# Column tiles of 32 for all full products of a two-layer attention and expert kernel, with a new order of steps

## The chip, the cores and the metric

The kernel runs on one core of one Trainium2 chip. The metric is the device time of one execution in microseconds (us), the median over several runs. In the trace TensorE's work is shown as PE (products) and PEld (weight loads), VectorE as DVE, ScalarE as ACT, GpSimd as POOL and SyncE as SP.

## The reference

The input is x, 4 batches x 512 tokens x 128 channels, f32. Two layers follow, each with attention of 16 heads of 8 channels and a mixture of 8 experts:

```python
xn = _layernorm(x, axis=-1)
x = x + _L0_attn_ref(xn, ...) + _L0_ffn_ref(xn, ...)      # causal attention; block_fwd: norm, causal attention, norm, 8 experts
xn = _layernorm(x, axis=-1)
x = x + _L1_attn_ref(xn, ...) + _L1_ffn_ref(xn, ...)      # attention without a mask; top-2 of 8 experts
```

So each batch has three attentions (0 and 1 causal, 2 without a mask). The expert part of layer 0 sends all 512 tokens through all 8 experts (128 to 512 channels, GELU, 512 to 128) and weights the results with the gates, zero outside the top two. That of layer 1 has experts 128 to 128 to 128.

## The kernel before

A batch is handled as 4 tiles of 128 tokens. Activations live turned as well (`normed_T_*`, channels on partitions, 512 tokens in the free dimension). PSUM has 8 banks of 128 x 512 f32: seven are handed out to steps, the eighth (`sum_bank`) sums the heads.

All engines follow one list of steps. `SCORE` is a string of letters, each the next step of a chain (A: load, norms, turns and projections; F, G: norms and gates around the experts; K: filling the stacks; L: expert weights; M: row maxima; T: turn of the maxima; S: scores; V: values; H: heads; E and O: experts of layer 0, in and out; I and J: those of layer 1), and a digit behind a letter is the PSUM bank of that step. `plan` turns it into the list, and each engine's block goes through the list and issues what it has to do for a step, with semaphores between engines. So the string sets the order on every engine and on every DMA queue at once. Three queues take DMAs: SyncE's (most), ScalarE's and GpSimd's (parts of the first stacks).

An attention runs like this. `project` makes queries and keys, which are split into three bf16 parts; `stack` copies the parts by DMA into `q_stack` and `k_stack`, two slots each. A `max` step (L877, with L882 adding the causal mask) multiplies a 64-row half of the stack for two heads at a time, two products side by side in 64-row tiles of the array (form `64*128` in the trace), and VectorE takes the negated maximum of each row (L535). `max_turn` (L890) turns the maxima with TensorE, VectorE copies them (L545), and a DMA (L1159) puts them into the stack. A `scores` step (L904, also `64*128`) makes the scores turned, ScalarE exponentiates them (L778), GpSimd cuts the causal triangle (L1071), and `values` (L925) multiplies with the values: four products side by side, each with 32 output rows (form `128*32`).

All other products use the full array (`128*128`): `project` (L854, L857), `out_project` (L935), `route` (L945, 8 columns), `expert_in` (L973, 512 columns), `expert_out` (L986, 128 columns), and the turns of f32 tiles by TensorE's transpose (L841). The bias product `route_bias` (L960) has 8 rows. The trace shows each f32 product as two products with a weight load each; an order of the program lists it once. The last pieces of the first stack (attention 0 of batch 0) are issued by GpSimd; the first `max` step waits for them. `load_experts` (L1117) brings a quarter of the expert weights in two DMAs of 512 KB.

## Time and profile before

| | |
|---|---|
| runs | 742.81, 741.61, 742.12 us; median 742.12 |
| profiled execution | 742.59 us, its span 740.0 us |
| granted TensorE clock, mean | 0.987 |
| PE busy | 711.5 us, 96%, 6222 products |
| PEld busy | 387.6 us, 52% |
| DVE busy | 569.5 us, 77% |
| ACT busy | 509.3 us, 69%; 63 table loads in the steps, 1.28 us each |
| POOL busy | 185.2 us, 25% |
| expert weights | DMAs of 512 KB, 4.9 and 6.7 us to landing |

The span is the time from the first to the last instruction of the program; some 2.6 us of an execution lie around it. Products are pipelined, so a row's duration is longer than the distance to the next start; how long TensorE is held by a group is read from the start of the group to the start of the next one.

### The profile page before, as it was taken

The numbers are of one execution on the slowest core, as the hardware profiler recorded it, in microseconds if no ns is written. First come the engines' busy times: TensorE is split into PE (matmuls) and PEld (weight loads), VectorE is DVE, ScalarE is ACT, GpSimd is POOL, SyncE is SP. The second block draws the span as 40 slices with busy tenths as digits, with TensorE's granted clock in tenths as the row PEclk, the third lists the DMA queues.
The fourth block names the chain that finished last, engine by engine and source line by source line (L and its number), as shares of the span: only waits on it lengthen the run. The fifth ranks groups of instructions, "written<-read, shape, count | busy, mean of one in ns | idle before, by whom it ended". The sixth has DMA issues, their size and how long they took to land.

```text
span 740.0 us, 15886 instructions
## 1 busy us (share of the span) xinstructions
PE 711.5 (96%) x6222; PEld 387.6 (52%) x6222; DVE 569.5 (77%) x1127; ACT 509.3 (69%) x632; POOL 185.2 (25%) x425
## 2 busy tenths in 40 slices
PE   5689999999999999999999999999999999999997
PEld 2333345667645665564544456567654666533345
DVE  5989998545788868688999967658778476788966
ACT  7266777366686567667789866764787748588882
POOL 5165546011343012103533200021372110010000
PEclk9699999999999999999999999999999999999999
DMA  6243523000132000004232200031031000030101
GB/s 155 53 140 129 164 93 110 11 19 1 34 96 79 3 25 17 19 5 111 64 88 69 62 3 19 4 99 31 5 93 54 9 11 17 3 94 13 28 25 39
DMA packets 42009, 38.75 MB, mean 52 GB/s; under 512 B 14312, under 2 KB 37232, under 8 KB 41712
## 3 DMA queue, kind: packets, MB, share of 16 engines
q1 hardware_dynamic: 40592, 36.17, 17.5%
q10 hardware_dynamic: 1152, 1.05, 0.6%
q8 instruction: 49, 0.80, 0.5%
q0 software_dynamic: 192, 0.52, 0.3%
q14 instruction: 24, 0.20, 0.1%
HBM read 10.47 MB, written 1.44 MB: 16 GB/s over the span
## 4 chain that ended last, share of the span: by engine, by line
PE 79%; DVE 9%; ACT 4%; DMA 4%; issue 2%; POOL 1%; SPq 1%; ACTq 1%; POOLq 0%; DVEq 0%
PE psum L986 19%; PE psum L973 18%; PE psum L925 15%; PE psum L904 8%; PE psum L877 8%; DVE neg_max L535 6%; PE psum L854 2%; PE psum L935 1%; PE psum L882 1%; DMA inverses<-heads_den 1%; PE psum L857 1%; PE psum L945 1%; PE psum L960 1%; ACT k_stack L716 1%; DVE acc L690 1%
## 5 line engine op out<-in xcount | busy, mean ns | idle before, releaser
L535 DVE TENSOR_REDUCE neg_max<-psum 128x2 f32<-128x1024 f32 (+2 forms) x320 | 344.9, 1113 | 82.2 <-PE psum L877 40.2
L778 ACT ACTIVATE probs<-psum 128x1024 f32<-128x1024 f32 (+1 forms) x320 | 287.1, 938 | 122.4 <-PE psum L904 120.7
L802 ACT ACTIVATE probs<-psum,col 128x512 f32<-128x512 f32 x160 | 100.5, 684 | 78.9 <-PE psum L973 78.3
L925 PE MATMUL psum<-probs,v_ones 128*32 128x512 f32 (+3 forms) x1536 | 152.8, 496 | 0.1
L986 PEld LDWEIGHTS psum<-ew,probs 128*128 128x128 f32 x1024 | 120.1, 192 | 17.6 <-issue 14.2
L986 PE MATMUL psum<-ew,probs 128*128 128x128 f32 x1024 | 129.1, 280 | 0.0
L877 PE MATMUL psum<-k_stack,q_stack 64*128 64x512 bf16 (+3 forms) x768 | 113.7, 333 | 13.6 <-DMA q_stack<-part 8.2
L1071 POOL TENSOR_SCALAR_AFFINE_SELECT probs<-probs 128x512 f32<-128x512 f32 x128 | 82.0, 646 | 176.7 <-ACT probs L778 176.6
L973 PE MATMUL psum<-normed_T_a,ew 128*128 128x512 f32 x256 | 118.0, 599 | 0.0
L904 PE MATMUL psum<-q_stack,k_stack 64*128 64x512 bf16 (+3 forms) x768 | 109.2, 330 | 3.9 <-DVE neg_max L535 1.2
L690 DVE SCALAR_TENSOR_TENSOR acc<-psum,gate,acc 128x128 f32<-128x128 f32 x256 | 71.9, 344 | 23.5 <-PE psum L986 21.7
L1057 POOL CAST max_part<-neg_max 128x16 bf16<-128x16 f32 x48 | 9.8, 205 | 298.2 <-DVE neg_max L535 282.8
L730 ACT ACT_TABLE_LOAD x63 | 80.8, 1283 | 1.1
L877 PEld LDWEIGHTS psum<-k_stack,q_stack 64*128 64x128 bf16 x768 | 36.5, 94 | 76.3 <-issue 24.8
L904 PEld LDWEIGHTS psum<-q_stack,k_stack 64*128 64x128 bf16 x768 | 31.7, 94 | 75.9 <-ACT probs L778 28.4
L973 PEld LDWEIGHTS psum<-normed_T_a,ew 128*128 128x128 f32 x256 | 45.6, 190 | 48.0 <-issue 42.9
L925 PEld LDWEIGHTS psum<-probs,v_ones 128*32 128x32 f32 x1536 | 35.8, 108 | 48.5 <-issue 33.2
L882 PEld LDWEIGHTS psum<-above,pick 64*128 64x128 bf16 x1024 | 44.9, 97 | 16.9 <-issue 1.4
L882 PE MATMUL psum<-above,pick 64*128 64x64 bf16 x1024 | 52.4, 193 | 0.0
L986 PEld LDWEIGHTS psum<-wout,probs 128*128 128x128 f32 x256 | 31.1, 191 | 8.2 <-issue 5.2
L986 PE MATMUL psum<-wout,probs 128*128 128x128 f32 x256 | 35.1, 282 | 0.0
L1040 POOL TENSOR_TENSOR part<-rest,part 128x512 bf16<-128x512 f32 x24 | 27.4, 1157 | 12.8 <-ACT part L759 11.6
(124 smaller groups left out, 494.2 us busy)
## 6 DMA issues: line engine op xcount, KB each, us to landing
q_stack<-part SPq DMA_DIRECT2D x66, 128.0 KB, 2.4
k_stack<-part SPq DMA_DIRECT2D x66, 128.0 KB, 2.4
heads_raw<-head_sums SPq DMA_DIRECT2D x24, 128.0 KB
heads_inv<-inverses SPq DMA_DIRECT2D x12, 256.0 KB, 3.3
ew<-w_expert_in SPq DMA_DIRECT2D x4, 512.0 KB, 4.9
ew<-w_expert_out SPq DMA_DIRECT2D x4, 512.0 KB, 6.7
q_stack<-k_stack SPq DMA_DIRECT2D x14, 128.0 KB, 2.3
q_stack<-maxT SPq DMA_DIRECT2D x48, 32.0 KB, 1.8
```

Of the source, the lines that this page charges most:

```text
L535: eng.tensor_reduce(neg_max[:, q % 2, :, xs[0]:xs[-1] + 1, i], src, AX_X, ALU.max, negate=True).then_inc(vector_done.sem, 1)
L690: eng.scalar_tensor_tensor(out=acc_of[b % 2][:, t, :], in0=src[:, t * P:(t + 1) * P], scalar=gate_of[layer][:, t, expert:expert + 1], in1= ...
L730: eng.preload_act_table(table)
L778: eng.activation(dst, src, ACT.Exp, scale=SCALE).then_inc(probs_ready.sem, 1)
L802: ins = eng.activation(probs[:, order.slot[step[:-1]], 2 * k + f, :], two_banks(step)[:, f, :], ACT.Gelu_apprx_tanh if layer else ACT.Gelu ...
L877: ins = eng.matmul(dst[:, a, col0:col0 + keys], q_stack[slot][rows_of, head, i * P:(i + 1) * P], k_stack[slot][rows_of, head, 0:keys], sta ...
L882: ins = eng.matmul(dst[:, a, col0:col0 + HALF], pick[rows_of, upper, :], above[rows_of, upper, :], start=False, stop=upper == 1)
L904: ins = eng.matmul(dst[:, a, n * width:(n + 1) * width], k_stack[slot][rows_of, head, j * P:(j + 1) * P], q_stack[slot][rows_of, head, TIL ...
L925: ins = eng.matmul(sum_bank[32 * c:32 * c + V_COLS, q0:TILES * P], v_ones[u][:, j, g // 2 * QH + c, col0:col0 + V_COLS], probs[:, order.sl ...
L973: ins = eng.matmul(dst[:, f, :], w, normed_T["y" if layer else "a"][:, :], start=True, stop=True)
L986: ins = eng.matmul(dst[:, t * P:(t + 1) * P], middle[:, f, t * P:(t + 1) * P], w, start=f == chunks[0], stop=f == chunks[-1])
L1071: eng.affine_select(out=diagonal, in_=diagonal, compare_op=ALU.is_ge, fill=no_chance, base=0, pattern=[[0, QH], [1, P]], channel_multiplie ...
```

## The change

A helper `columns` issues a product as four, one for each 32 columns of the kept operand, each into its own 32 partitions of the same PSUM bank. All products of the full array go through it, except the transposes of f32 tiles and the bias product of 8 rows. The turn of the maxima, a bf16 transpose until now, becomes such a product with the identity, with an f32 result, which VectorE copies to bf16. The string `SCORE` is new; its first line stands for it here.

```diff
+COLUMN = 32
+COLUMN_TILES = P // COLUMN
 SCORE = """
-AAAAAAAA6A6A0AAAKAKAKA1M2M4M0M2M4M0A6M2M4T6M0M2M4A6S0S2M4S0A6S2M4S0M2VKKAM0S4T6M2AVM0AVAM4M2A6S0M4LS2VM0T6S2AM4S0KM2
...
+AAAAAAAA6A6A0KAAKAALAKA1M2M4M0M2M4M0A6M2M4T6M0M2M4LA6S0M2S4M0A6M4AS2S0AM2AVKT6M0M4S2VM0AS2A6KS4M0M2VAS4T6KM0S2M4S0AM
...
@@ vector, max_turn
-                    src = bank(step)[:, 0:P // 2].bitcast(BF16)
+                    src = bank(step)[:, 0:P]
@@ tensor
+            def columns(dst, kept, moving, start=True, stop=True):
+
+                for c in range(COLUMN_TILES):
+                    some = slice(COLUMN * c, COLUMN * c + COLUMN)
+                    ins = eng.matmul(dst[some, :], kept[:, some], moving, start=start, stop=stop)
+                return ins
+
@@ project
-                        ins = eng.matmul(dst, proj_qk[:, u, k, :], src[:, :], start=True, stop=True)
+                        ins = columns(dst, proj_qk[:, u, k, :], src[:, :])
                     else:
                         for t in range(TILES):
-                            ins = eng.matmul(dst[:, t * P:(t + 1) * P], src[:, t * P:(t + 1) * P],
-                                             projs[:, u, 0, :], start=True, stop=True)
+                            ins = columns(dst[:, t * P:(t + 1) * P], src[:, t * P:(t + 1) * P], projs[:, u, 0, :])
@@ max_turn
-                    dst = bank(step)[:, 0:P // 2].bitcast(BF16)
+                    dst = bank(step)[:, 0:P]
                     eng.wait_ge(max_split.sem, 4 * (q + 1))
-                    eng.transpose(dst, max_part[:, q % 2].rearrange("p a n c -> p (a n c)"),
-                                  ident16[:, :]).then_inc(work_full.sem, 1)
+                    ins = columns(dst, max_part[:, q % 2].rearrange("p a n c -> p (a n c)"), ident16[:, :])
+                    ins.then_inc(work_full.sem, 1)
@@ route (out_project alike)
-                        ins = eng.matmul(dst[:, t * EXPERTS:(t + 1) * EXPERTS], src[:, t * P:(t + 1) * P],
-                                         router[:, layer, :], start=True, stop=True)
+                        ins = columns(dst[:, t * EXPERTS:(t + 1) * EXPERTS], src[:, t * P:(t + 1) * P], router[:, layer, :])
@@ expert_in
-                        ins = eng.matmul(dst[:, f, :], w, normed_T["y" if layer else "a"][:, :], start=True, stop=True)
+                        ins = columns(dst[:, f, :], w, normed_T["y" if layer else "a"][:, :])
@@ expert_out
-                            ins = eng.matmul(dst[:, t * P:(t + 1) * P], middle[:, f, t * P:(t + 1) * P], w,
-                                             start=f == chunks[0], stop=f == chunks[-1])
+                            ins = columns(dst[:, t * P:(t + 1) * P], middle[:, f, t * P:(t + 1) * P], w,
+                                          start=f == chunks[0], stop=f == chunks[-1])
```

How the order moves is shown at two places. The first is SyncE's queue at the start, behind the loads of x and of the small weights (`q_stack0` and `part0` belong to attention 0, `q_stack1` and `part1` to attention 1, `maxT` is the turned maxima, `ew1` and `ew2` the expert weights). Before:

```order
L1128 DMA q_stack0<-k_stack0 16x4096 x2
L382 DMA q_stack0<-part0 16x8x512 x3
L382 DMA k_stack0<-part0 16x8x512 x3
L1159 DMA q_stack0<-maxT 16x8x128
L1128 DMA q_stack1<-k_stack1 16x4096 x2
L382 DMA q_stack1<-part1 16x8x512 x3
L382 DMA k_stack1<-part1 16x8x512 x3
L1159 DMA q_stack0<-maxT 16x8x128
L1117 DMA ew1<-w_expert_in 128x1024
L1117 DMA ew2<-w_expert_out 128x1024
```

And now:

```order
L1134 DMA q_stack0<-k_stack0 16x4096 x2
L384 DMA q_stack0<-part0 16x8x512 x3
L384 DMA k_stack0<-part0 16x8x512 x3
L1123 DMA ew1<-w_expert_in 128x1024
L1123 DMA ew2<-w_expert_out 128x1024
L1165 DMA q_stack0<-maxT 16x8x128
L1123 DMA ew1<-w_expert_in 128x1024
L1123 DMA ew2<-w_expert_out 128x1024
L1134 DMA q_stack1<-k_stack1 16x4096 x2
L384 DMA q_stack1<-part1 16x8x512 x3
L384 DMA k_stack1<-part1 16x8x512 x3
```

Two pairs of expert weights have moved ahead: one from behind the second maxima to in front of the first, one more in front of the second stack.

The second place is TensorE among the last experts of batch 0 and the first attention steps of the next (L986 and L973 are expert products, L877, L882 and L904 row-paired ones of maxima and scores). Before:

```order
L986 MATMUL psum<-ew,probs 128x128 x8
L904 MATMUL psum<-q_stack,k_stack 128x256 x4
L877 MATMUL psum<-k_stack,q_stack 128x512 x2
L882 MATMUL psum<-above,pick 128x64 x4
...
L986 MATMUL psum<-ew,probs 128x128 x16
L973 MATMUL psum<-normed_T_a,ew 128x512 x4
L986 MATMUL psum<-ew,probs 128x128 x8
L890 MATMUL psum<-ident,max_part 128x128
```

And now (L834 is the helper's line, L933 the values, L885, L890 and L912 the row-paired ones):

```order
L834 MATMUL psum<-ew,probs 32x128 x32
L834 MATMUL psum<-normed_T_a,ew 32x512 x16
L933 MATMUL psum<-probs,v_ones 32x128 x4
L834 MATMUL psum<-ew,probs 32x128 x32
L912 MATMUL psum<-q_stack,k_stack 128x512 x2
L912 MATMUL psum<-q_stack,k_stack 128x384 x2
L885 MATMUL psum<-k_stack,q_stack 128x512 x2
L890 MATMUL psum<-above,pick 128x64 x4
L834 MATMUL psum<-ew,probs 32x128 x32
```

Eight full products have become 32 narrow ones, and a value step now stands between two expert steps, where before the form of the array changed at each such border. Over the whole program the row-paired products are followed by others 258 times before and 240 times now. Passages between full and `128*32` products number 36 before and 14 now. The program holds 4470 products before and 7470 now, which are 6222 and 12078 with f32 products counted twice.

## Rows read from the trace of the kernel before

**Rows 1.** The page: busy time, share of the span and instructions of each engine.

```profile
PE 711.5 (96%) x6222; PEld 387.6 (52%) x6222; DVE 569.5 (77%) x1127; ACT 509.3 (69%) x632; POOL 185.2 (25%) x425
```

**Rows 2.** Stages: start:end, us, busy (count) of each engine, clock, DMA share, GB/s.

```profile
0.00:120.00 120.00, 97.97 (x1165) 0.93 0.44 125
120.00:740.00 620.00, 613.58 (x5061) 1.00 0.14 38
...
60.00:100.00 40.00, 37.24 (x515) 15.64 (x507) 38.84 (x60) 27.47 (x35) 20.76 (x43) 1.00 0.47 145
```

**Rows 3.** TensorE's timeline at seven places: start us, us, what, number of products.

```profile
313.77 1.07 PE L925 MATMUL psum<-probs,v_ones 128*32 128x512 f32 x8
314.77 0.34 PE L877 MATMUL psum<-k_stack,q_stack 64*128 64x384 bf16 x2
...
205.06 2.36 PE L925 MATMUL psum<-probs,v_ones 128*32 128x512 f32 x32
207.35 0.39 PE L877 MATMUL psum<-k_stack,q_stack 64*128 64x512 bf16 x2
...
322.28 1.16 PE L935 MATMUL psum<-projs,headsT 128*128 128x128 f32 x8
323.37 0.39 PE L904 MATMUL psum<-q_stack,k_stack 64*128 64x512 bf16 x2
...
306.62 0.23 PE L882 MATMUL psum<-above,pick 64*128 64x64 bf16 x4
306.79 2.05 PE L986 MATMUL psum<-ew,probs 128*128 128x128 f32 x16
308.77 0.39 PE L904 MATMUL psum<-q_stack,k_stack 64*128 64x512 bf16 x2
...
299.70 3.60 PE L973 MATMUL psum<-normed_T_a,ew 128*128 128x512 f32 x8
303.23 0.23 PE L877 MATMUL psum<-k_stack,q_stack 64*128 64x128 bf16 x2
303.29 0.22 PE L882 MATMUL psum<-above,pick 64*128 64x64 bf16 x4
303.35 0.22 PE L877 MATMUL psum<-k_stack,q_stack 64*128 64x128 bf16 x2
...
133.85 2.05 PE L986 MATMUL psum<-ew,probs 128*128 128x128 f32 x16
135.74 0.59 PE L973 MATMUL psum<-normed_T_a,ew 128*128 128x512 f32 x1
...
124.81 0.95 PE L945 MATMUL psum<-router,normed_T_a 128*128 128x8 f32 x8
125.70 0.23 PE L877 MATMUL psum<-k_stack,q_stack 64*128 64x128 bf16 x2
```

**Rows 4.** The first stack: SyncE's timeline, the chain of work, who waited.

```profile
13.48 2.07 SPq L382 DMA_DIRECT2D k_stack<-part  x3
...
17.20 3.64 DMA q_stack<-part
...
PE psum L877 <- DMA q_stack<-part: 8.2, 1, 8.2
```

**Rows 5.** Stack pieces (L382) issued from 33 to 40 us, then from 40.3 to 45.

```profile
DMA to landing us min/median/max: 2.3/2.4/2.5
...
DMA to landing us min/median/max: 4.8/5.3/7.2
```

**Rows 6.** The page, DMA queues: TensorE's code (packets, MB, share of 16 engines).

```profile
q8 instruction: 49, 0.80, 0.5%
```

**Rows 7.** One stage of TensorE alone, columns as in the second group.

```profile
353.30:356.50 3.20, 3.19 (x66) 1.00 0.09 18
```

**Rows 8.** TensorE's timeline at the first maxima; 24 products start between these rows.

```profile
20.98 0.29 PE L877 MATMUL psum<-k_stack,q_stack 64*128 64x128 bf16 x2 [8.19 <-DMA q_stack<-part]
...
22.01 0.53 PE L877 MATMUL psum<-k_stack,q_stack 64*128 64x384 bf16 x2
```

More of the change, by code:

```diff
@@ new lines @@
+2VM4S0VAAM2M0S4AS2VS4T6M0S2VVM4M2AS0S4S0M2S4AVS0M4S2VM0VT6LAVM2S4S0VM4A6S0M2M4S0A6S0S2VHM4VVT2M0S4M2A6S4S0AVM2S4M0HA
+VAM2S4M0VS4KKM2S0VT6M4KS2M0M4VS2M0S4VS2HHM0M4VVS0T6M2S4M0M2S4VHLM0S4HS2VM4S0M2VS4T6VM0M2S4H6S0M4VS2M0VM4S2HM0VVM4S2H
+T6A0S4A6S2M0S4VS2HM0M4S2A6S0S2VM4M0VHHS2T6HA4S2S0VAAH6VFM2FS0S4VVVAS0A6S2M4S0VKF2M0M4AVE2E0F6KKM4M2AM0FFVAAO6E4OF4E2
+E0O6AM4M2M0OE4T0E2E0T6M4M2O6M4M0M2OLE4E0E2AO6M4M0S2OE2E4T6M0M2O6S4AM0M2OE4E0VO6S2S4M0OE2O6S0S4M2OO0HOS2M4F6S2S0VVFVV
+M4FS2S0A6VHT2S4S0F3VHM4S2S0F6F4S2HS0FVG6S2S0FM4HVFF6HVS2M0S4VH6S2S0FS4KVKVT6A2I0FI4HA6VS2S0KM4VF6S2M4S0VF6S2FM4M0GVF
@@ new lines @@
+AVE2E4E0M2M4O6M0AS2M4AOVS0M2M4VT6E0GE2KVE4M0M2O6S4M0M2OM4M0E2O6M4M0S2OA2S4S0A6VS2M4M0A6J2A3E4J6T2I0M4M2J6I0G2VS4AM2H
+M0O6M2M4M0OE2AE4E0E2F6J0S4M2O6KM0S4M2OS0S4M2VAVS0KHM4S2F6M0M4S2VM0S2HVT6M4S0M2VS4M0A6S2S4AAM0VT6M2S0S4J6VM2M0S4T6VS2
+M4S0G6S2M4VM0S2M4J6S0S2AS4VE0AAVE2T6M4M0O6S2M4HM0OS2S4AS0VO6M2S4M0HVM2S4M0OS4M2S0KVM4KS0H6KM2M0AM4HJ6E2E0J2HVT6M4S0M
+2O6HM0S4S2OS4S0M2VT6S4VVS2FM0S4VM2FS4S0VVS2M4HS0F6M2S4VT0F6S4M2S0VF6S4S0M2VHT4VFHA6S0S2FKM4VVM0S2FM4H6S0M2KGS4VVM0HS
+4M2VG6S4M0HKS2VT6M4S2GM0VS4M2HA6VS0S4S2VVM0S4A6S2S4M0HVS2VHT6VM4S0HS2F6VS0M4S2H6S0M4S2VVS0M4FS2VVM0S4M2VAI4FI0KAF6M2
@@ new lines @@
+M4AVHE0F6VM2M4FE0T6FE2KE4HM0M2O6M4S0KM2OS4HM0GE2I4I0T6A2VM4S0M2J6E4M0M2O6M4M0S2OS4M2S0VJ6S4M0S2VJ6J0S4M2O6M0S4M2OS0M
+4HM2VE0G6F2E4J6E0M2M4HJ6E0T4J5VM2S0M4J6S2M0S4VA6S2S4M0VA6S2S0S4VO6T4M2S0S4OHM2S0S4VA6S0S4M2AVVM0S4M2VM0M4S2VT6S0M2S4
+H6S0M2VS4M0M2O6S0M4M2HOS0S4VVT6M2HS0S4G6S0AM2E4E0E2M4AM0VVS4M2S0F6S4KKM2M0KHHVO6M4M2M0HOE4HE2T6E0T6M4M2VVM0M4S2O6M0S
+2S4OS0S2M4VH6T2VVS0M4M2O6S4S0S2OS4HS0S2FVA6S4M0VVFS2M4S0VVM2S0F6S4S2M0VT6VM4S0M2VAF6M4HHS0HI2F6AFI0M4M2GG6VS0M4HS2FF
+F6S0S2M4KHVT6VVS0M4S2H6S0S4VKS2FKM0FS4VS2VVS0M4S2VF6M0S2M4VE2T6F0E4E2VM0M4FFO6M2M0S4OE4E2O6OVM0M4E2F6E0E4E2O6M0M4S2O
@@ L118 @@
+S0M2S4VE0O6T0M4S2M0OS4M2M0VE4GO6M2M0HM4GOE2E0T2VVE4M0HM2O6M4HHM0S2OE4HE2O6HS0S4M2OM0S2M4VO6M2S0M4OH0S2S4F6S0S2FVT6FI
+4I0F6VM2S4S0F6VS2M4S0F6FVM2S4S0J6FKVS4FM2S0KKJ6S4M2VS0S4J6VT0M2S4J6S0M2S4VG6S0M4VM2M0HS4J6S2S4VM0S2VM4M0I2M4G6M0M2I4
+M0VM2S4M0T6VS2M4S0M2S4M0VS2M4VHM0S2M4F6S0S2M4S0T6HVS2M4M0VS2M4VS0M2HJ6S4S0M2VHT6S4M0HS2VS4M0S2VM4S0H6S2M4S0VM2S4VS0M
+2S4J6VS0S2HS4T6VJ6GS0VS2S4S0VG6S2GS4GVJ6S0S2S4VVJ2VHJ6I0HHI4G6J0J6HJ1J0HG6J1H0G
 """
@@ L934, in _ @@
                     for t in range(TILES):
-                        ins = eng.matmul(dst[:, t * P:(t + 1) * P], headsT[:, t * P:(t + 1) * P],
-                                         projs[:, step[2], 1, :], start=True, stop=True)
+                        ins = columns(dst[:, t * P:(t + 1) * P], headsT[:, t * P:(t + 1) * P], projs[:, step[2], 1, :])
                     ins.then_inc(work_full.sem, 1)
```

19 lines of the change are left out of this document (removed).

## Prediction

> **What bounds the kernel now.** I read the page's busy line first. TensorE is busy 96% of the span over 6222 products, VectorE 77%, ScalarE 69% [rows 1]. One long stage view then splits the span. Up to 120 us TensorE is idle for 22 us and its granted clock is 0.93 on average; from 120 to 740 us it is busy 613.6 of 620 us at full clock [rows 2]. So after 120 us only TensorE's own work sets the time. Before that VectorE does: it is busy 38.8 of 40 us between 60 and 100 us [rows 2].
>
> A busy TensorE is not all streaming. The starts in its timeline give four prices [rows 3]. (1) **A column run.** Eight value products of 512 columns take 1.00 us to the next start, and the chain of 32 (512, 384, 256 and 128 columns) 2.29 us. The second holds 768 columns more, so a column costs 1.29/768 = 1.68 ns for both passes of the four tiles together. 512 columns are 0.86 us, which leaves 0.14 us for leaving the run. (2) **A full run of 128 columns.** Eight products 1.09 us, sixteen 1.98: 0.111 each, and 0.20 for leaving. (3) **A full run of 512 columns.** Eight take 3.53 us; at 0.43 each (half of 0.86) the run leaves at 0.09. (4) **Entering** from the row-paired products: four of 64 columns take 0.17 us instead of about 0.06, so some 0.10, ahead of either kind. So the same product streams equally long in both forms; what differs is the edge of a run.
>
> **The change part by part**, all of it after the counts of the two orders and with these prices.
>
> *Leaving full runs.* 131 times a full product is followed by a row-paired one; 109 of these leave from f32 products. They pay 0.09 to 0.20, in the middle of their kinds 0.16; a column run pays 0.14. 109 x 0.02 = 2.2 us won (between -5 and +6.5). The other 22 leave from the turned maxima; I count them at nothing.
>
> *Fewer runs.* The orders hold 258 entries into f32 or turned work before and 240 now: 18 round trips x (0.10 + 0.14) = 4.3 us.
>
> *Values beside expert steps.* 36 passages between full and column form become 14, since only the f32 turns and the bias products stay full: 22 x 0.14 = 3.1 us.
>
> *Boundaries inside a run.* Sixteen expert products take 1.89 us when a 512-column product follows, 0.11 more than 16 x 0.111 [rows 3]. Some boundaries show that, others nothing; with half of it the 130 of them cost 7.2 us. In column form the chain of 32 fits its slope with none at all; I take 0.017 for each of 232, 3.9 us. Won 3.3 us.
>
> *The rate of 128-column products.* The order holds 640 expert-out products and 96 of the projections, each of two passes in the trace, so 1472, which go from 0.111 each to a quarter of a group. The slope gives 0.215 us for a pair of passes against 0.223; won 0 to 5.5 us, I take 3.
>
> *The router.* Eight products of 8 columns take 0.89 us [rows 3], as long as if each had 128 columns. In narrow columns each step issues 32 short ones. The nearest row is four products of 64 columns in 0.06 us [rows 3], 0.015 each, so 0.5 us for the step: 8 steps x 0.4 = 3.2 us won. The other end is no gain. The Trainium skill (TensorE: Matmul & The Clock Gate, "Wait — 56ns, not 53.3ns?") states that starts never come closer than about 25 ns; by it a router step would take 0.8 us and this term would be about 0.7 us. The timeline's four starts in 0.06 us are closer than that.
>
> *The copies of the maxima* read f32 instead of bf16, 48 of them at about 0.2 us; VectorE waited before many of them, so nothing. ScalarE loads its tables as often as before.
>
> The sum of TensorE's terms is 2.2 + 4.3 + 3.1 + 3.3 + 3 + 3.2 = 19.1 us.
>
> **What does not reach the end.** Work before 120 us is paced by VectorE and by the first transfers, so the roughly 1.5 us of these terms that lie there are lost. A TensorE that is 3% shorter meets VectorE sooner in the attention stages; the idle that TensorE has after 120 us is 6.4 us [rows 2], and I add a quarter of that, 1.5 us.
>
> **What the new order adds.** SyncE now issues the first expert weights (two transfers of 512 KB) right behind its own pieces of the first stack, and the second pair right behind the first maxima; before, one pair was issued near 40 us. TensorE waits 8.2 us for the last pieces of that first stack; GpSimd issues the last at 17.20 us and it lands 3.64 us later [rows 4]. SyncE has issued its own pieces by 15.6 us, so the weights go into the engines just ahead of them. The trace has this collision at another place: stack pieces issued beside the weights at 40 to 45 us took 4.8 to 7.2 us to land, those issued from 33 to 40 us 2.3 to 2.5 [rows 5]. So +2.4 to +4.8 us; at the start the pieces are slowed already, so it could also be less: 0 to 5, I take 3. Nothing hides it, since the first maxima, and all of VectorE's chain behind them, wait for that landing. Once the start is late it stays so.
>
> **Sum.** The profiled execution took 742.6 us, 2.6 of them outside its span of 740.0. 742.6 - 19.1 + 1.5 + 1.5 + 3 = 729.5; the median of the runs is 0.5 below the profiled execution, so **729 us**.
>
> **Rivals.**
>
> *A. The pieces are dearer or cheaper than taken, nothing else* (forecast, 0.60).
>
> *B. More is won: about 718 us* (0.17). If every full run left at 0.20, every inner boundary cost 0.11 and the rate term were 5.5, TensorE would win 9 us more, and with the first landing not delayed 12. For it: 128-column runs do pay 0.20. Against it: the 512-column runs pay half of that.
>
> *C. VectorE takes the gain: about 738 us* (0.12). It has 569 us of work, and in the attention stages it is as busy as TensorE. The new order puts expert steps elsewhere; if it leaves VectorE short of slots in two stages, some 6 us of TensorE's gain turn into waits for the maxima, and the start costs its 5. Against it: TensorE idles 1% after 120 us today.
>
> *D. The supply of products fails: slower, above 744 us* (0.08). The orders give 12078 products on TensorE instead of 6222. An expert-out step of 16 products becomes 64, each with its weight load, in 1.75 us: 27 ns a pair. Of these there are 5888. If a pair takes 2.2 ns longer than that, the 13 us are gone; from 30 ns on the kernel is slower, and at 35 ns it takes 776 (5888 x 8 ns more than forecast). For it: the densest long stretch today is 66 products in 3.2 us, 48 ns each [rows 7], and the code that is fetched, 49 blocks now [rows 6], about doubles, so nothing here shows a sustained 27 ns. Against it: by the slope above the chain of 32 value products ends with eight at this spacing, and the first maxima start 24 products in 1.03 us right after the 8.2 us wait, with no gap beyond their streaming [rows 8].
>
> *E. The sequencer needs a fixed time for each product* (0.03, in place of a part of D). The Trainium skill (the same page, the same section) gives about 62 ns for one when decoding is done in microcode. As a mechanism here: 64 products would bind at that spacing instead of 27 ns, 5888 x 35 ns = 206 us, so about 935 us. The 24 products in 1.03 us [rows 8] are 43 ns each and the 66 in 3.2 us [rows 7] 48 ns, closer than such a spacing allows, unless they were queued before.
>
> **How the numbers follow.** Two results closer than 0.2% (1.5 us) can't be told apart here. A and B are faster, C mostly (738 lies beyond 740.6), D and E slower; of A and C a strip reaches no change. Faster 0.86, same 0.04, slower 0.10. The range leaves out D, E and the best of B: from 742.1 less 26 to 742.1 less 3, **716 to 739**.
>
> **What the profile after would show.** Right: 16 expert-out products in column form in 1.72 to 1.76 us inside a long run, value and expert groups with no gap between them, router steps near 0.5 us, idle after 120 us below 9 us, and the first L877 product's successor at 23 to 24 us instead of 21. Wrong: expert-out steps above 1.9 us inside a run (D), a first wait that still ends at 21 us (then 726), VectorE's maxima behind many TensorE waits after 120 us (C), or a granted clock below 1.00 after 120 us, which none of today's stages shows.

## The result and the profile after

The change is faster, by half of what was forecast: 735.79 us, median of 18 runs (732.62 to 741.07), against 742.62 us for the kernel before on the same chips (18 runs, 740.42 to 744.06). The ratio is 0.9911, 95% interval [0.9896, 0.9925], so 6.6 us won (5.6 to 7.7) where the working had 13.1. The profiled execution took 735.74 us with a span of 733.8 us.

| | before | after |
|---|---|---|
| span of the profiled execution | 740.0 | 733.8 |
| PE busy | 711.5 | 695.9 |
| PE idle until 120 us | 22.0 | 24.0 |
| PE idle after 120 us | 6.4 | 13.9 |
| start of the first maxima | 20.98 | 24.31 |

The page of the changed kernel, engines, then TensorE's code, answering to [rows 1, 6]:

```profile
PE 695.9 (95%) x12078; PEld 348.7 (48%) x12078; DVE 577.4 (79%) x1127; ACT 509.2 (69%) x632; POOL 185.7 (25%) x425
...
q8 instruction: 95, 1.56, 0.9%
```

TensorE is busy for 15.6 us less, yet the span fell by 6.2 only. The stages say where the rest went; they answer to [rows 2], with the same columns (count in brackets, the granted clock behind POOL):

```profile
0.00:120.00 120.00, 96.01 (x1366) 42.80 (x1370) 104.75 (x189) 76.52 (x110) 58.11 (x137) 0.90 0.41 114
120.00:740.00 620.00, 599.86 (x10720) 305.87 (x10712) 472.69 (x939) 432.64 (x524) 127.54 (x289) 0.99 0.15 42
```

The second window ends with the span at 733.8, so TensorE is idle for 613.8 - 599.9 = 13.9 us in it. Split further, before and then after, from 120 us on (the sixth attention starts at about 303 us before and 296 us after; 16 of the expert products of 512 columns, 6.9 us, stood before that place and stand behind it now, so compare the idle of these windows and not their lengths):

```profile
120.00:135.00 15.00, 14.93 (x147) 9.08 (x140) 11.26 (x28) 9.65 (x13) 6.42 (x15) 1.00 0.15 41
135.00:303.00 168.00, 167.85 (x1196) 102.11 (x1194) 116.39 (x266) 107.98 (x137) 34.32 (x71) 1.00 0.12 31
303.00:740.00 437.00, 430.80 (x3722) 231.98 (x3721) 337.51 (x642) 314.31 (x372) 84.52 (x200) 1.00 0.15 41
```

```profile
120.00:135.00 15.00, 11.97 (x198) 5.56 (x194) 11.42 (x20) 8.02 (x12) 7.79 (x17) 0.89 0.29 81
135.00:296.00 161.00, 160.14 (x3084) 88.49 (x3076) 115.99 (x255) 106.83 (x135) 30.70 (x62) 1.00 0.14 37
296.00:733.80 437.80, 427.75 (x7448) 211.81 (x7446) 345.29 (x667) 317.79 (x378) 89.05 (x210) 1.00 0.16 42
```

Idle went from 0.1 to 3.0, from 0.15 to 0.9 and from 6.2 to 10.1 us. Between 120 and 135 us the longest are two waits for VectorE, 1.04 us for `normed_a` at 123.21 us and 1.55 us for `neg_max` at 125.79 us. Late in the second wait, from 125.4 to 128.8 us, the granted clock is at half. Later there are many short ones.

```profile
123.21 0.66 PE L850 MATMUL psum<-ident,normed_a 128*128 128x128 f32 x4 [1.04 <-DVE normed_a L450]
125.79 0.61 PE L885 MATMUL psum<-k_stack,q_stack 64*128 64x512 bf16 x2 [1.55 <-DVE neg_max L537]
```

TensorE's own prices, at five places that answer to [rows 3] (start us, us, what, number of products):

```profile
134.04 1.93 PE L834 MATMUL psum<-ew,probs 128*32 128x128 f32 x64
135.78 1.90 PE L834 MATMUL psum<-normed_T_a,ew 128*32 128x512 f32 x16
...
315.69 1.90 PE L834 MATMUL psum<-normed_T_a,ew 128*32 128x512 f32 x16
317.41 1.04 PE L933 MATMUL psum<-probs,v_ones 128*32 128x512 f32 x8
318.27 1.90 PE L834 MATMUL psum<-normed_T_a,ew 128*32 128x512 f32 x16
319.98 0.24 PE L834 MATMUL psum<-ident,max_part 128*32 128x128 bf16 x4
...
320.73 1.95 PE L834 MATMUL psum<-ew,probs 128*32 128x128 f32 x64
322.62 0.39 PE L912 MATMUL psum<-q_stack,k_stack 64*128 64x512 bf16 x2
...
277.11 7.05 PE L834 MATMUL psum<-normed_T_a,ew 128*32 128x512 f32 x64
...
131.69 0.46 PE L834 MATMUL psum<-router,normed_T_a 128*32 128x8 f32 x32
132.08 0.23 PE L885 MATMUL psum<-k_stack,q_stack 64*128 64x128 bf16 x2
```

The expert-out step of 64 products takes 135.78 - 134.04 = 1.74 us ahead of a column group, where the forecast had 1.75. The eight values between two expert groups take 0.86 us (318.27 - 317.41), exactly the slope of the prediction with no border on either side. Leaving for a row-paired product costs 0.15 (322.62 - 320.73 = 1.89). A router step takes 0.39 us, forecast 0.5, before 0.89.

To see the sum I took every group of like products in the trace, from its start to the next group's start, and split the distance into streaming (products by their slope), border (the median rest of that kind of passage) and wait (what a passage takes beyond that median, if over 0.06 us). A stretch at half clock falls under wait.

| us | before | after | difference | forecast |
|---|---|---|---|---|
| streaming | 617.1 | 606.9 | -10.1 | -6.2 |
| borders | 75.4 | 66.5 | -8.9 | -12.9 |
| both | | | -19.0 | -19.1 |
| waits until 135 us | 35.3 | 39.3 | +4.0 | +4.5 |
| waits after 135 us | 5.8 | 14.6 | +8.8 | +1.5 |

(The groups that the split can't sort leave 0.2 us.) The sum is -6.2 us, the span's. The rows are less exact than their sum: with slopes and medians taken in another way the same rule gives -9.3 for streaming, -11.3 for borders, +7.4 for the waits until 135 us and +6.8 for those after. The split also cuts at 135 us where the forecast of +4.5 and +1.5 cuts at 120. The windows need no such choice: TensorE's idle rises by 2.0 us until 120 us and by 7.5 us after it, 2.9 of them from 120 to 135 us. So TensorE's terms came as priced in their sum, the first maxima were late as priced, and **the waits after 120 us took five times what they were given**.

The start of the first maxima, in the chain of work and in TensorE's timeline, answering to [rows 4, 8]:

```profile
17.98 6.19 DMA q_stack<-part
...
24.31 0.29 PE L885 MATMUL psum<-k_stack,q_stack 64*128 64x128 bf16 x2 [10.54 <-DMA q_stack<-part]
```

The last piece of the first stack took 6.19 us instead of 3.64. It was also issued 0.8 us later; an earlier half-clock stretch in this execution (from 9.3 us) is the likely reason. The first maxima start 3.3 us late.

### The profile page after: what moved, and what is told of

The parts are those of the page before. It is cut to its first block, busy times and chain, and to the rows that moved or that the text cites. A ratio compares the mean times of both kernels' runs of the same rounds, so it can differ in the third digit from the quotient of the medians.

```text
span 733.8 us, 27594 instructions
## 1 busy us (share of the span) xinstructions
PE 695.9 (95%) x12078; PEld 348.7 (48%) x12078; DVE 577.4 (79%) x1127; ACT 509.2 (69%) x632; POOL 185.7 (25%) x425
## 4 chain that ended last, share of the span: by engine, by line
PE 78%; DVE 13%; ACT 3%; issue 3%; DMA 2%; POOL 1%; SPq 0%; ACTq 0%; DVEq 0%; POOLq 0%
PE psum L834 43%; PE psum L933 14%; PE psum L885 8%; PE psum L912 8%; DVE neg_max L537 6%; ACT probs L780 2%; PE psum L890 1%; DMA q_stack<-part 1%; DVE acc L692 1%; PE psum L850 1%; PE psum L966 1%; PE psum L959 1%; DMA q_stack<-maxT 0%; DVE part L484 0%; ACT probs L804 0%
## 5 line engine op out<-in xcount | busy, mean ns | idle before, releaser
L933 PE MATMUL psum<-probs,v_ones 128*32 128x512 f32 (+3 forms) x1536 | 156.7, 496 | 0.3 <-POOL probs L1077 0.2
L885 PE MATMUL psum<-k_stack,q_stack 64*128 64x512 bf16 (+3 forms) x768 | 114.0, 334 | 19.3 <-DMA q_stack<-part 11.4
L834 PE MATMUL psum<-ew,probs 128*32 128x128 f32 x4096 | 124.1, 274 | 0.0
L834 PEld LDWEIGHTS psum<-ew,probs 128*32 128x32 f32 x4096 | 109.7, 110 | 18.6 <-issue 14.7
L834 PE MATMUL psum<-normed_T_a,ew 128*32 128x512 f32 x1024 | 117.7, 595 | 0.4 <-ACT probs L804 0.4
L912 PE MATMUL psum<-q_stack,k_stack 64*128 64x512 bf16 (+3 forms) x768 | 107.1, 328 | 5.5 <-DVE neg_max L537 2.2
L692 DVE SCALAR_TENSOR_TENSOR acc<-psum,gate,acc 128x128 f32<-128x128 f32 x256 | 71.9, 343 | 27.1 <-PE psum L834 26.0
L885 PEld LDWEIGHTS psum<-k_stack,q_stack 64*128 64x128 bf16 x768 | 36.8, 95 | 88.9 <-issue 25.5
L912 PEld LDWEIGHTS psum<-q_stack,k_stack 64*128 64x128 bf16 x768 | 31.1, 94 | 72.8 <-ACT probs L780 23.7
L834 PEld LDWEIGHTS psum<-normed_T_a,ew 128*32 128x32 f32 x1024 | 31.9, 110 | 62.6 <-issue 54.5
L933 PEld LDWEIGHTS psum<-probs,v_ones 128*32 128x32 f32 x1536 | 35.4, 108 | 39.2 <-issue 30.1
L890 PEld LDWEIGHTS psum<-above,pick 64*128 64x128 bf16 x1024 | 45.2, 97 | 16.9 <-issue 2.0
L890 PE MATMUL psum<-above,pick 64*128 64x64 bf16 x1024 | 52.5, 193 | 0.0
L834 PE MATMUL psum<-wout,probs 128*32 128x128 f32 x1024 | 33.6, 274 | 0.0
L834 PEld LDWEIGHTS psum<-wout,probs 128*32 128x32 f32 x1024 | 27.1, 110 | 11.6 <-issue 6.1
```

The source lines that it names most:

```text
L692: eng.scalar_tensor_tensor(out=acc_of[b % 2][:, t, :], in0=src[:, t * P:(t + 1) * P], scalar=gate_of[layer][:, t, expert:expert + 1], in1= ...
L834: ins = eng.matmul(dst[some, :], kept[:, some], moving, start=start, stop=stop)
L885: ins = eng.matmul(dst[:, a, col0:col0 + keys], q_stack[slot][rows_of, head, i * P:(i + 1) * P], k_stack[slot][rows_of, head, 0:keys], sta ...
L890: ins = eng.matmul(dst[:, a, col0:col0 + HALF], pick[rows_of, upper, :], above[rows_of, upper, :], start=False, stop=upper == 1)
L912: ins = eng.matmul(dst[:, a, n * width:(n + 1) * width], k_stack[slot][rows_of, head, j * P:(j + 1) * P], q_stack[slot][rows_of, head, TIL ...
L933: ins = eng.matmul(sum_bank[32 * c:32 * c + V_COLS, q0:TILES * P], v_ones[u][:, j, g // 2 * QH + c, col0:col0 + V_COLS], probs[:, order.sl ...
```

## Experiments

The theory after this result, called S: the gain is whole on TensorE, 3 to 4 us are lost at the start to the early expert weights, and the rest is lost because a shorter TensorE waits for the maxima and exponentials of the attention stages. Rivals: the new order does it (O), or the expert work of VectorE and ScalarE, which stands between the attention steps on their queues (W).

**1. Tiles without the order, the order without tiles, the loads late, a bf16 turn.** All against the change, but order_alone, which is the kernel before with the new `SCORE`. tiles_alone is the change with the old `SCORE`. The two smaller edits (of `SCORE` only its first two lines change):

```diff
@@ SCORE, loads_late
-AAAAAAAA6A6A0KAAKAALAKA1M2M4M0M2M4M0A6M2M4T6M0M2M4LA6S0M2S4M0A6M4AS2S0AM2AVKT6M0M4S2VM0AS2A6KS4M0M2VAS4T6KM0S2M4S0AM
-2VM4S0VAAM2M0S4AS2VS4T6M0S2VVM4M2AS0S4S0M2S4AVS0M4S2VM0VT6LAVM2S4S0VM4A6S0M2M4S0A6S0S2VHM4VVT2M0S4M2A6S4S0AVM2S4M0HA
+AAAAAAAA6A6A0KAAKAAAKA1M2M4M0M2M4M0A6M2M4T6M0M2M4A6S0M2S4M0A6M4AS2S0AM2AVKT6M0M4S2VM0AS2A6KS4M0M2LVAS4T6KM0S2M4S0AM2
+VM4S0VAAM2M0S4AS2VS4T6M0S2VVM4M2AS0S4S0M2S4AVS0M4S2VM0VT6LLAVM2S4S0VM4A6S0M2M4S0A6S0S2VHM4VVT2M0S4M2A6S4S0AVM2S4M0HA
@@ max_turn, maxturn_bf16
-                    dst = bank(step)[:, 0:P]
-                    ins = columns(dst, max_part[:, q % 2].rearrange("p a n c -> p (a n c)"), ident16[:, :])
+                    dst = bank(step)[:, 0:P // 2].bitcast(BF16)
+                    for c in range(COLUMN_TILES):
+                        some = slice(COLUMN * c, COLUMN * c + COLUMN)
+                        ins = eng.transpose(dst[some, :], max_part[:, q % 2].rearrange("p a n c -> p (a n c)")[:, some],
+                                            ident16[:, :])
```

Expected, tiles_alone:

> The new column products with the old order of steps. Theory (TensorE wins 19 us in all, the new order spends 6 of it in waits, half of that at the start): without the 4.3 us of fewer runs and the 3.1 us of values beside expert steps TensorE wins 11 to 12 us, the first maxima start at 21 us again, so 742.6 - 11.5 + 1 to 2 of new waits = 732 to 733, faster than the whole change (735.8). Rival (the new order is what pays, column products alone cost switches that the old order did not foresee): 738 to 741, slower than the whole change.

Expected, order_alone:

> The new order with the old full products. It has about 100 more passages between values and full products than the column form needs, at 0.14 to 0.20 us each against 0.02. Theory: no gain of the column form (15 us of the 19), some 4 us won by 18 fewer round trips, 3.3 lost at the start, 10 or more lost at values beside expert steps: 748 to 756. Rival (the order itself carries the gain): 736 to 740.

Expected, loads_late:

> The whole change, but the first two pairs of expert weights are issued where the old order issued them (behind the second maxima, and with the third pair). Theory (the last pieces of the first stack land late because 1 MB of weights is ahead of them, and the delay reaches the end): they land 2.5 us earlier, the first maxima start near 21.7 us, total 733 to 733.5, 2.5 us under the change. Rival (the lost start is absorbed by VectorE's and the later waits): total unchanged within 0.7 us though the first maxima start earlier.

Expected, maxturn_bf16:

> The whole change, but the turn of the maxima is four column transposes with a bf16 result, so that VectorE copies bf16 again. Theory (VectorE's copy grew from 0.218 to 0.282 us, 48 times, and VectorE is close to the bound): 3.1 us less of VectorE's work, of which a third to a half shows, 734.5 us. Rival (the copy was hidden): 735.8, no change.

Borders and waits are those of the split above, in us over the whole program.

| | us, median | ratio to before | first maxima | borders | waits |
|---|---|---|---|---|---|
| tiles_alone | 735.0 | 0.989 [0.9863, 0.9917] | 20.7 | 71.9 | 49.3 |
| order_alone | 751.88 | 1.0119 [1.0092, 1.0146] | 24.8 | 81.1 | 44.4 |
| loads_late | 731.88 | 0.9847 [0.9822, 0.9873] | 20.6 | 66.4 | 49.2 |
| maxturn_bf16 | 735.18 | 0.9894 [0.9865, 0.9923] | 23.6 | 67.0 | 51.6 |

The tiles alone give 7.6 us, the order alone costs 9.3. tiles_alone lies between its theory (732 to 733) and its rival (738 to 741), order_alone where the theory had it, and loads_late won more than its theory had (733). In the full form the order has 5.7 us more in borders (81.1 against 75.4), since values then stand between full products; in column form it has 5.4 us less (66.5 against 71.9). So the order only makes sense with the tiles. The windows of tiles_alone, old order, show that the waits after 135 us come with the tiles and not with the order:

```profile
135.00:303.00 168.00, 167.31 (x3182) 90.97 (x3182) 118.37 (x268) 108.62 (x139) 34.37 (x71) 1.00 0.12 33
303.00:734.60 431.60, 422.12 (x7276) 206.31 (x7268) 338.10 (x642) 313.46 (x371) 84.54 (x200) 1.00 0.16 42
```

From 303 us on TensorE is idle for 9.5 us here, 10.1 in the change, 6.2 before. From 120 to 135 us it is the other way round; first tiles_alone, then order_alone:

```profile
120.00:135.00 15.00, 14.48 (x276) 7.50 (x270) 10.80 (x27) 11.39 (x16) 6.69 (x16) 1.00 0.12 34
120.00:135.00 15.00, 13.02 (x136) 7.40 (x129) 11.90 (x20) 9.83 (x14) 9.65 (x18) 1.00 0.38 106
```

TensorE is idle here for 0.5 us with the tiles alone and for 2.0 with the order alone, 0.1 before and 3.0 in the change. In loads_late, whose start is not late, it is still 2.2 us, so these waits belong to the order itself. Over the whole stretch behind 120 us the idle is 6.4 us before, 10.7 with the tiles alone, 8.0 with the order alone and 13.9 with both: the tiles bring 4.3 of the 7.5 us, the order on top of them 3.2. Rival O falls as the main cause, but holds for that part. loads_late shows the price of the start: 3.9 us less than the change by the medians, 4.8 by the ratios, and its chain of work has this in place of the 6.19 us:

```profile
17.76 2.66 DMA q_stack<-part
```

The bf16 turn is within its scatter of the change (0.6 us, intervals overlap), between its theory (734.5) and its rival (735.8). Its copies are back to the time of before; these are the rows of VectorE by form, of the kernel before and of the change:

```profile
L545 DVE COPY maxT<-psum 128x128 bf16<-128x128 bf16 x48 | 10.3, 218 | 19.0 <-PE psum L890 19.0
```

```profile
L547 DVE CAST maxT<-psum 128x128 bf16<-128x128 f32 x48 | 13.5, 282 | 16.9 <-PE psum L834 16.8
```

A copy of f32 takes 282 ns instead of 218, 3.1 us over all. The Trainium skill (VectorE: DVE Perf Modes, "Why PSUM operands drop a tier") says that a PSUM operand allows at most the double rate, and f32 only the single one; the two rows agree in direction, the f32 copy takes longer.

**2. The expert work of VectorE and of ScalarE (rival W).** Each edit was made in both kernels. In *_dve the weighted additions of the experts cover 32 of their 128 columns, in *_act every GELU is an exponential, so no table loads stand between the steps.

```diff
@@ before_dve, after_dve
-                            out=acc_of[b % 2][:, t, :], in0=src[:, t * P:(t + 1) * P],
+                            out=acc_of[b % 2][:, t, 0:32], in0=src[:, t * P:t * P + 32],
@@ before_act, after_act
-                                             ACT.Gelu_apprx_tanh if layer else ACT.Gelu, bias=col[:, c:c + 1])
+                                             ACT.Exp, bias=col[:, c:c + 1])
```

Expected, before_dve:

> The kernel before, with VectorE's 256 weighted additions of expert results cut to 32 of 128 columns (three quarters of each are left out). VectorE has 25 to 40 us less to do, all of it after 120 us. Theory (in the old kernel TensorE is late, VectorE is not: 5.8 us of waits after 135 us, 2.5 of them for VectorE): 740.5 to 742, at most 2 us faster. Rival (VectorE is a general brake): 736 or less.

Expected, after_dve:

> The changed kernel with the same cut of VectorE's weighted additions. Theory (the faster TensorE has turned part of its gain into waits for VectorE: 7 of the 14.6 us of waits after 135 us): 729 to 731.5, 4 to 7 us under the change, so more than the cut brings the kernel before. Rival (the waits are latency of chains, maxima to turn to DMA to scores, which lighter additions don't shorten): 734.5 to 736.

Expected, before_act:

> The kernel before, with exp in place of both GELUs, so that all but one of ScalarE's 64 table loads (1.28 us each) are gone. Theory (TensorE is late, ScalarE is not, 1.5 us of its waits after 135 us are for ScalarE): 740.5 to 742. Rival: 738 or less.

Expected, after_act:

> The changed kernel with exp in place of both GELUs and so without the table loads. Theory (4.0 us of the new waits after 135 us are for ScalarE's exponentials, which stand behind table loads): 731.5 to 733.5, 2 to 4 us under the change. Rival (VectorE alone sets those waits, ScalarE only ends last by a little): 735 to 736.

Measured: before_dve 741.27 us, 0.9988 [0.9969, 1.0007]; after_dve 733.67 us, 0.9881 [0.9856, 0.9906]; before_act 741.12 us, 0.9982 [0.9963, 1.0002]; after_act 734.65 us, 0.9888 [0.9861, 0.9914]. The change gains 2.1 us from a VectorE that has 25 us less to do, and 1.1 us from a ScalarE without table loads; the kernel before gains about 1 us from either. TensorE's waits after 135 us stay at 13.1 and 13.6 us (14.6 in the change). Both results of the change lie between theory and rival, nearer to the rivals. Rival W falls as the main cause: how full these engines are with expert work is not what most of TensorE's waits hang on.

**3. The attention work itself.** From the sixth attention on, the row maxima go over half of the keys (*_max), the exponentials over half of each block (*_exp), or both (*_both); the other half of the results is left out, and TensorE's work stays.

```diff
@@ vector, max
+                    if ATTENTIONS.index((b, u)) >= 5:
+                        src = src[:, :, :, 0:keys // 2]
@@ scalar, scores
+                    if ATTENTIONS.index((b, u)) >= 5:
+                        some = slice(0, width // 2)
+                        dst, src = (dst[:, :, :, some], src[:, :, :, some]) if len(xs) > 1 else (dst[:, :, some], src[:, :, some])
```

Expected, before_both:

> The kernel before with the same two halvings from the same attention on. Its TensorE waits 5.1 us after that place. Theory: 3 to 4 us less, 738 to 740, which is 6 us less than the changed kernel gains by the same cut; that difference is the part of TensorE's gain that the attention stages took back. Rival: it gains as much as the changed kernel, 733 to 735, and the cut tells nothing of the change.

Expected, after_both:

> The changed kernel; from attention 1 of batch 2 on (296 us of the profile) VectorE takes the maxima over half of the keys and ScalarE exponentiates half of each score block (the other halves are left out); TensorE's work and the order are the same. Theory (the new waits sit in the attention stages, where a maximum of 1.22 us or an exponential of 1.02 us follows on every 0.3 us of products, and not in VectorE's or ScalarE's expert work): TensorE's waits after 296 us, 12.5 us in the changed kernel, fall to 2 or 3, total 725.5 to 727.5. Rival (they are latency of semaphores and transfers, in either kernel): 733 or more.

Expected, after_max:

> The changed kernel with only the maxima halved from that attention on. Theory (both engines end waits in turn): 3 to 6 us less than the change, 730 to 733. Rival (VectorE alone is the brake): as after both cuts, 725.5 to 727.5.

Expected, after_exp:

> The changed kernel with only the exponentials halved from that attention on. Theory (both in turn): 2 to 5 us less than the change, 731 to 734. Rival (VectorE alone): 735 to 736, unchanged.

Measured: before_both 739.17 us, 0.9961 [0.9946, 0.9977]; after_both 730.62 us, 0.9865 [0.9839, 0.9891]; after_max 735.24 us, 0.9912 [0.9895, 0.9929]; after_exp 735.2 us, 0.9915 [0.9893, 0.9938]. One stage shortened gives nothing that can be told from the change (0.9911), where both theories had 2 to 6 us and VectorE as the only brake had 725.5 to 727.5 for after_max; both together give 5.2 us by the medians but 3.4 by the ratios, between theory and rival; the kernel before gains 2.7 and 2.9. TensorE's idle behind 296 us is 7.1 us in after_both (431.2 - 424.1), against 10.1 in the change. That favours S without showing it, since the intervals allow equal gains. So the edit was made stronger, `// 4` in place of `// 2` in both engines, beside the change itself on one chip.

Expected, after_again:

> The change itself once more, so that the two kernels with short attention work can be compared with it on one chip: 735.8 us, between 734.5 and 737.

Expected, after_quarter:

> As after_both, but from the sixth attention on the maxima go over a quarter of the keys and the exponentials over a quarter of each block. Theory (a shorter TensorE waits for the attention stages of VectorE and ScalarE): TensorE's idle time behind 296 us falls from 10.1 us to 6 or less, and the change gains 6 to 7 us against itself, 729.5 us. Rival (what waits is the fixed latency of the chain, semaphores, loads, transfers and the small steps between the stages): no more than with half the work, 3 to 4 us, 732 us, idle near 7 us.

Expected, before_quarter:

> The same edit in the kernel before. Theory: TensorE there has little idle time that hangs on these stages (6.2 us behind 303 us, 5.2 with half the work), so at most 3 us are won, 739.5 us, and the distance between the two kernels grows from 6.6 to about 10 us. Rival: both kernels gain the same, within 1 us, and the attention stages don't explain why the change gained only half.

Measured: after_again 735.41 us, 0.991 [0.9889, 0.9932]; after_quarter 731.03 us, 0.9852 [0.983, 0.9874]; before_quarter 738.69 us, 0.995 [0.993, 0.9969]. The change gains 4.4 us, the kernel before 3.2 (741.86 - 738.69): a difference of 1.2 us where the rival said within 1 and the theory 3 or more. By the ratios the gains are 4.3 and 3.7 us, 0.6 apart, and the intervals allow equal ones: the times side with the rival. The last window, of after_again, then of after_quarter:

```profile
293.00:740.00 447.00, 429.44 (x7480) 213.16 (x7479) 346.85 (x668) 319.18 (x380) 89.67 (x213) 1.00 0.15 42
```

```profile
293.00:740.00 447.00, 426.54 (x7490) 211.54 (x7486) 214.34 (x669) 212.49 (x380) 89.52 (x213) 0.99 0.15 42
```

VectorE has 132 us less to do and ScalarE 107, and TensorE's idle is 9.5 us (731.9 - 293 - 429.4) and 9.4 us (728.9 - 293 - 426.5). The forecast of S, 6 or less, is wrong. TensorE's span in this window is 3.0 us shorter all the same, and its busy time falls by 2.9 us with the same products: rows of pipelined products overlap short waits, so such waits stand in the busy time and not in the idle. By the split of the first section, with each wait put down to the semaphore that came last, the waits in this stretch are:

| us behind 293 or 303 us | before | before_quarter | after_again | after_quarter |
|---|---|---|---|---|
| exponentials and maxima | 2.8 | 0.5 | 5.4 | 1.1 |
| splits (`rest`), `headsT`, stack transfers | 1.1 | 1.5 | 3.2 | 5.2 |
| all other and not named | 1.2 | 0.9 | 3.3 | 2.1 |
| sum | 5.1 | 2.9 | 11.9 | 8.4 |

So of the 6.8 us that the change waits longer here, 2.6 are waits for maxima and exponentials. With these stages short such waits nearly go (5.4 to 1.1), but 2.0 us return at the next link, the splits of queries and keys and the transfers that open each attention. The traces give S this part of 2.6 us; the times don't show it, since the kernel before gains nearly as much from the same cut. Shortening these stages doesn't return what the change lost: by this table at least a part of the waits moves to the next link of the chain.

**4. What is left: the start, the clock, the copies.** late_bf16 is loads_late with the bf16 turn; late_warm adds 28 products of zeros into the first maxima's bank, ahead of TensorE's first long wait; one_early takes only the pair of weights in front of the first maxima out of its early place; a pair follows ahead of the V steps, near 40 us.

```diff
@@ late_warm, first max step
+                            bank_free(step)
+                            for _ in range(28):
+                                eng.matmul(one_bank(step), zeros[:, 0:P], zeros[:, :], start=True, stop=True)
@@ SCORE, one_early
-AAAAAAAA6A6A0KAAKAALAKA1M2M4M0M2M4M0A6M2M4T6M0M2M4LA6S0M2S4M0A6M4AS2S0AM2AVKT6M0M4S2VM0AS2A6KS4M0M2VAS4T6KM0S2M4S0AM
+AAAAAAAA6A6A0KAAKAAAKA1M2M4M0M2M4M0A6M2M4T6M0M2M4LA6S0M2S4M0A6M4AS2S0AM2AVKT6M0M4S2VM0AS2A6KS4M0M2LVAS4T6KM0S2M4S0AM
```

Expected, late_bf16:

> The two small edits that made the change faster are put together: the first two pairs of expert weights issued where the old order had them, and the turned maxima written as bf16 by four column transposes. Theory 1 (the start decides): the late loads gave 3.9 us, and the bf16 turn by itself 0.6 us although its profile showed a first stack that still took 6.4 us to land; its copies are 48 x 0.06 us shorter on VectorE, which sets the end only where TensorE waits for it. Expected 731.2 us (730.3 to 732.2), ratio about 0.9845. Rival (the copies of the maxima stand in the chain of waits after 135 us): all 48 copies count, 3 us off the loads_late result, 729 us.

Expected, late_warm:

> late_bf16 with 28 products of zeros in the bank of the first maxima while TensorE waits for the first stack, so that the engine is not idle before it. Theory (the clock lost by waiting costs time at the start): in the change the granted clock is half from 16 to 37 us, and with late loads from 16 to 27 and 30 to 33 us; TensorE is busy about half of that time, so if its work were on the path, half of 14 us x 0.5 busy = 3 to 4 us could come back: 728 us. Rival (until 120 us VectorE and the transfers set the pace, as the prediction says, and a slow TensorE lies beside them): within 1 us of late_bf16, 730.5 to 732 us, with the clock column of 16 to 36 us higher.

Expected, one_early:

> Only the pair of expert weights that the new order issues behind the first maxima stays early but is put ahead of the second stack alone; the pair ahead of the first maxima goes, so that nothing is issued beside the last pieces of the first stack; the next pair follows near step 61. Theory (the price is the first pair, beside the first stack): the first maxima start at 21 us, and the result is that of loads_late, 732 us (731 to 733), ratio about 0.986. Rival (the second pair, beside the second stack, costs too: its pieces took 4.6 to 5.6 us in the change): the second attention starts 1.5 us later than with late loads, 733.5 to 734.5 us.

late_bf16 took **729.68 us**, 0.9844 [0.9819, 0.9869], the fastest version that computes everything, 12.5 us faster than the kernel before by the medians. It lies between the theory's 731.2 and the rival's 729, but its ratio is that of loads_late (0.9847), so the copies of the maxima have no effect that these runs show.

late_warm took 733.9 us, 0.9891 [0.9866, 0.9915], slower than late_bf16 by 4.2 us. Its windows, and then rows of its timeline, the last at the place where it loses:

```profile
12.00:20.00 8.00, 6.64 (x48) 2.85 (x37) 3.73 (x16) 4.89 (x19) 4.58 (x5) 1.00 0.94 214
24.00:34.00 10.00, 8.45 (x82) 3.82 (x84) 9.96 (x13) 1.29 (x2) 0.82 (x4) 0.50 0.13 30
```

```profile
12.42 6.22 PE L878 MATMUL psum<-zeros 128*128 128x512 bf16 x28
...
77.02 0.39 PE L918 MATMUL psum<-q_stack,k_stack 64*128 64x512 bf16 x2 [2.44 <-DMA q_stack<-maxT]
```

The zeros kept the clock full from 12 to 20 us and nearly so to 24 (0.97) (late_bf16: 0.68 from 12 to 20 us, 0.50 from 20 to 24), and the seventeenth reduction of maxima started at 40.7 us, against 40.2 in late_bf16: nothing won, since VectorE is busy 9.96 of the 10 us from 24 to 34 us. The half-clock stretch moved, from 15 to 32 us to 24 to 34 us, and is shorter (10.2 us for 17.1). So at the start the clock costs nothing that can be seen. What late_warm loses stands at other places, as far as the one profiled execution shows (736.2 us, where that of late_bf16 took 729.1): at 77 us TensorE waits 2.44 us for turned maxima whose DMA took 5.67 us (issued at 71.30 us, behind four transfers of expert weights issued from 63.7 to 66.4 us). One of these transfers took 10.4 us to land. In late_bf16 they stand on the queue 0.7 to 1.4 us earlier, the maxima land in 2.8 us, and there is no such wait. Behind it come two half-clock stretches of 3.4 us, from 78.4 and from 126.2 us, that late_bf16 doesn't have; each can cost up to 1.7 us. The same collision as at the start, met by chance. Both expectations, 728 and 730.5 to 732, missed this.

one_early took 733.38 us, 0.9882 [0.986, 0.9904]. Its first maxima start at 20.8 us as with late loads, but the second attention's first reduction starts at 52.3 us, against 49.9 in loads_late and 53.5 in the change. Its stack pieces from 33 to 60 us took this long to land, and those of loads_late this, in this order:

```profile
DMA to landing us min/median/max: 4.0/4.9/6.3
```

```profile
DMA to landing us min/median/max: 2.3/2.8/4.5
```

So both early pairs cost; the result is 0.1 us under the rival's range and outside the theory's. By the medians the first pair costs 2.4 us (735.8 against 733.4) and the one ahead of the second stack 1.5 (against 731.9); the ratios' intervals overlap, so this split is rough.

## Why the prediction was half right

The direction, the prices of TensorE and the late start came as forecast. The gain did not: 6.6 us instead of 13.1, and most of the missing 6.5 is one term of the sum, the idle that TensorE gains behind 120 us.

- **What bounds the kernel.** Right for the kernel before: TensorE is the bound after 120 us, and shortening VectorE's or ScalarE's work moves that kernel by 0.5% at most (before_quarter).
- **The prices of TensorE.** Right in their sum: streaming and borders fell by 19.0 us, forecast 19.1. That the two agree to 0.1 is luck: by the same split streaming fell by 10.1 (forecast 6.2) and borders by 8.9 (forecast 12.9), and the other way of taking the split gives 20.6 in all. The rate of 128-column products gave 92 groups of 16 x 0.04 = 3.6 us (forecast 3). The eight router steps fell from 0.89 to 0.99 us each to 0.27 to 0.51, about 4.5 us in all (forecast 3.2). Leaving full runs and the boundaries inside runs were together put a little high.
- **Values beside experts.** Right: 0.86 us for eight, and the order's borders change sign with the tiles (+5.7 us without them, -5.4 with them).
- **Rivals D and E.** Refuted. 64 products and loads in 1.74 us are 27 ns a pair, the 64 of 512 columns behind 277.11 us stream without a gap, and 95 packets of code instead of 49 left no trace in the times. The Trainium skill (TensorE: Matmul & The Clock Gate, "Wait — 56ns, not 53.3ns?") gives about 62 ns for a product when decoding is done in microcode; the row of 27 ns for a product and its load shows that no such spacing binds here.
- **The start.** Right: the first maxima came 3.3 us late (forecast 3), the last piece took 6.19 us to land (forecast range 6 to 8.4), and late loads return 3.9 us (4.8 by the ratios), more than the 3 that the sum had. That TensorE's gain before 120 us would be lost fits: its idle until 120 us rose.
- **The step that failed** is in "What does not reach the end": *"the idle that TensorE has after 120 us is 6.4 us [rows 2], and I add a quarter of that, 1.5 us."* That idle rose by 7.5 us, and the half-clock stretch from 125.4 to 128.8 us takes up to 1.7 us more in this execution. The 7.5 us have two parts. The tiles alone, in the old order, bring 4.3: this is the wait that the term stands for, and it is nearly three times as large. The new order adds 3.2, 2.5 of them from 120 to 135 us; the sum had no term for waits of the order behind 120 us, and took 120 us as the end of VectorE's full stretch, which in the change is still busy 4.00 of 4 us from 122 to 126 us. The idle of before measures how often TensorE waits now; it doesn't say how close behind it the other results arrive. As I read it, many inputs of a TensorE that was busy 99% had landed only just in time, so that a part of each gain became a wait at the next dependent step.
- **Signs.** One of the listed signs of being right is missing, an idle below 9 us after 120 us (13.9), and one of being wrong is there, a granted clock below 1.00 after 120 us. The expert step in 1.74 us and the values without a gap are as listed; the router step was put at 0.5 us and takes 0.39.
- **Rival C** had nearly the right time (738) and a part of the mechanism. It blamed the order and VectorE's maxima: the order brings 3.2 of the 7.5 us, and the longest wait there, 1.55 us, is for maxima. The larger part is there in the old order too (tiles_alone), and with VectorE's maxima alone cut to half nothing came back.
- **Rival B's sum** doesn't come out: with the prediction's own counts its three conditions give 109 x 0.04 = 4.4, 130 x 0.055 = 7.2 and 5.5 - 3 = 2.5, so 14 us more and not 9, and some 712 us with the first landing in time. The chances of D and E make 0.11 for slower, not 0.10. The forecast hangs on neither.
- **Open.** Behind the sixth attention's start the split counts 6.8 us more of waits than before (11.9 in after_again against 5.1): 2.6 for maxima and exponentials, 2.1 for splits, `headsT` and stack transfers, 2.1 for others and for those that the trace names no releaser for. Each is put down to the semaphore that came last, and no edit shows it as a cause. No run separates why the new order makes TensorE wait at 120 to 135 us, and none shortens the fixed steps between an attention's stages.

## What to carry to other kernels

When an engine that is busy 99% is made faster by 3%, the waits that it has today are no measure of the slack behind them: count how late the results arrive that it uses (here 7.5 of 19 us came back as idle behind the start, 4.3 with the tiles alone), and expect that shortening a stage of the chain behind it moves a part of the waits to the next link: either attention stage cut to half gave nothing, and both at a quarter of their work gave 4 us, nearly what the kernel before gained from the same cut. Keep bulk loads that nobody needs soon out of the queue near small transfers that somebody waits for; here two pairs of 1 MB cost 3.9 us, and moving them was worth half of what the tiles gave (7.6). A form change and an order of steps are one edit: the order cost 9.3 us without the form and gained 3.1 with it, once the loads were late.

## What the chip showed that I had not expected

- A column product with its weight load takes 27 ns in a long run (64 in 1.74 us, each pass of f32 counted as one); full f32 products of 8 columns took 0.111 us each, and in column form the step falls from 0.89 to 0.39 us. That is 32 starts at 12 ns each, across four column tiles, closer than the 25 ns that the rule in the prediction's router term allows.
- The granted clock went to half for some 3.4 us in the middle of steady work, behind a stretch of 4 us in which TensorE was busy 1.41 us only. The windows from 122 to 130 us of the change show the waits first and most of the slow clock (0.65, half until 128.8 us) behind them, while TensorE is already busy again. It is not in every execution: after_again has 3.0 us of idle between 120 and 135 us too, at a clock of 1.00.

```profile
122.00:126.00 4.00, 1.41 (x16) 0.76 (x14) 4.00 (x7) 1.74 (x2) 1.66 (x3) 0.92 0.60 165
126.00:130.00 4.00, 4.00 (x34) 1.21 (x34) 2.72 (x3) 0.00 (x0) 0.99 (x5) 0.65 0.00 0
```

- Keeping TensorE busy with zeros for most of a wait of 8 us did not save the clock: in late_warm it fell to half 3 us after the wait's end, at 23.8 us, for 10.2 us, with TensorE busy 1.83 of the 4 us from 20 to 24 us; without the zeros it was at half for 17.1 us.
